# GpSimd's gathers of an item's routed results: one unbroken group, behind a wait for the stacked queries of the item two ahead

## The reference, cut to what matters

```python
x = x + L0_ffn(L0_cond(x))     # pooling, then a mixture of 32 experts, 4 of them for each token
x = x + L1_ffn(L1_cond(x))     # a matrix chosen for each item, attention, then 8 experts, 2 for each token
# L1_ffn.block_forward, for each item:
h = layernorm(x, ln1_g, ln1_b)
q, k, v = split(h @ Wqkv)                       # 16 heads of 16
q, k = (rope(q), rope(k))
probs = softmax(causal(q @ k.T / sqrt(16)))
x = x + (probs @ v) @ Wproj
h2 = layernorm(x, ln2_g, ln2_b)                 # routed to 2 of 8 experts
```

## Time and profile before

| | us |
|---|---|
| median of 3 runs | 1644.0 (1638.05 to 1645.99) |
| the profiled execution, its own time | 1637.33 |
| its span, from the first to the last instruction | 1635.4 |
| TensorE's granted clock, mean over the span | 0.94 |

### The profile page before, as it was taken

How to read it: one execution, slowest core, us unless ns; L and a number is a source line. 1 busy time by engine, 2 the same in 40 slices (tenths; PEclk the granted TensorE clock), 3 DMA queues, 4 the chain that set the end, 5 groups by cost and what they waited for, 6 DMA issues and landing times.

```text
span 1635.4 us, 27565 instructions
## 1 busy us (share of the span) xinstructions
PE 1438.9 (88%) x9777; PEld 1247.0 (76%) x9777; DVE 1028.3 (63%) x2455; ACT 916.5 (56%) x2160; POOL 717.0 (44%) x710
## 2 busy tenths in 40 slices
PE   7997599999999997589978888879965999999996
PEld 5776599999999985466766666667744999999996
DVE  2998376776677767457766766757654555655552
ACT  5886255555555532267766666667844545554552
POOL 0787443344334114344444455553344444544443
PEclk9989799999999999799988999999976999999998
DMA  5411356555655531586576665566743223433312
GB/s 178 136 56 32 84 162 180 154 163 175 180 158 160 150 110 41 97 142 124 117 129 114 117 127 101 103 119 112 110 129 99 72 53 92 98 88 89 52 22 26
DMA packets 139448, 182.00 MB, mean 111 GB/s; under 512 B 22485, under 2 KB 107296, under 8 KB 139312
## 3 DMA queue, kind: packets, MB, share of 16 engines
q1 hardware_dynamic: 110512, 127.23, 31.3%
q0 software_dynamic: 28160, 51.96, 15.7%
q10 hardware_dynamic: 640, 1.05, 0.4%
HBM read 107.28 MB, written 42.08 MB: 91 GB/s over the span
## 4 chain that ended last, share of the span: by engine, by line
PE 64%; DVE 15%; another core or an unknown queue 8%; issue 6%; ACT 3%; POOL 2%; DMA 1%; SPq 1%; ACTq 0%; DVEq 0%; POOLq 0%
PE banks L942 40%; PE banks L1483 4%; PE banks L1440 4%; PE banks L451 3%; PE banks L1536 2%; PE banks L1004 2%; DVE X L1705 2%; DVE rm L1737 2%; DVE hidden L977 2%; DVE smax L1695 2%; PE banks L1496 1%; PE banks L1457 1%; DVE lo_w L911 1%; PE banks L1498 1%
## 5 line engine op out<-in xcount | busy, mean ns | idle before, releaser
L942 PE MATMUL banks<-hi_x,hi_w 128*128 128x320 f32 (+1 forms) x832 | 291.6, 350 | 36.5 <-DVE hidden L977 29.7
L942 PE MATMUL banks<-lo_x,hi_w 128*128 128x320 f32 (+1 forms) x832 | 286.5, 344 | 0.0
L942 PE MATMUL banks<-hi_x,lo_w 128*128 128x320 f32 (+1 forms) x832 | 286.1, 344 | 0.0
L942 PE MATMUL banks<-hi_w,hi_h 128*128 128x256 f32 x896 | 261.5, 292 | 6.8 <-issue 4.5
L884 POOL DMA_INDIRECT xe<-pooled,idx x160 | 155.7, 973 | 228.2 <-PE banks L1004 183.1
L942 PE MATMUL banks<-lo_w,hi_h 128*128 128x256 f32 x896 | 254.4, 284 | 0.0
L942 PE MATMUL banks<-hi_w,lo_h 128*128 128x256 f32 x896 | 254.2, 284 | 0.0
L942 PEld LDWEIGHTS banks<-hi_x,hi_w 128*128 128x128 f32 x832 | 158.9, 191 | 58.7 <-DVE hidden L977 33.4
L1896 POOL DMA_INDIRECT out<-X,tab x64 | 106.3, 1661 | 200.5 <-DVE X L1999 185.8
L1589 ACT ACTIVATE PN<-banks,smax 128x256 f32<-128x256 f32 (+1 forms) x512 | 180.7, 443 | 13.3 <-DVE smax L1695 13.2
L942 PEld LDWEIGHTS banks<-hi_w,hi_h 128*128 128x128 f32 x896 | 172.3, 192 | 8.4 <-issue 5.9
(11 more groups left out here) (187 smaller groups left out, 3100.7 us busy)
## 6 DMA issues: line engine op xcount, KB each, us to landing
w<-in_L_ffn_w SPq DMA_DIRECT2D x96, 256.0 KB, 5.6
done<-res SPq DMA_DIRECT2D x32, 640.0 KB
QS<-parts_qk SPq DMA_DIRECT2D x128, 128.0 KB
BIG<-in_L_ffn_W SPq DMA_DIRECT2D x16, 1024.0 KB
KS<-parts_qk SPq DMA_DIRECT2D x120, 128.0 KB
mask<-in_c_masks SPq DMA_DIRECT2D x16, 257.0 KB, 2.8
pooled<-XF SPq DMA_DIRECT2D x16, 256.0 KB, 3.2
WS<-in_L_cond_W SPq DMA_DIRECT2D x16, 256.0 KB
```

Of the source, the lines that this page charges most:

```text
L942: last = e.matmul(o, a[i], b[j], start=start and k == 0, stop=stop and k == 2, skip_group_check=True)
```

## The change

In `POOL_ROUND` the eight gathers of item i + 3 now stand behind both `entry` pairs, the rotation and `base`: six in one piece, then the two norms with one gather between them, and the last gather behind. Before the first gather of an item b (from the fourth item on) POOL also waits until `s_stack[0]` tells that the queries of item b - 2 have been stacked.

```diff
     POOL_ROUND = (
-        ("got", 2, 1, 3), ("entry", -3, 0), ("entry", -3, 1), ("qk", 1, 0), ("qk", 1, 1), ("entry", -3, 2),
-        ("got", 3, 0, 0), ("got", 3, 0, 1), ("got", 3, 0, 2), ("got", 3, 0, 3), ("entry", -3, 3),
-        ("got", 3, 1, 0), ("got", 3, 1, 1), ("base", -2), ("norm", -1, 1), ("got", 3, 1, 2), ("norm", 2, 0))
+        ("entry", -3, 0), ("entry", -3, 1), ("qk", 1, 0), ("qk", 1, 1), ("entry", -3, 2), ("entry", -3, 3),
+        ("base", -2), ("got", 3, 0, 0), ("got", 3, 0, 1), ("got", 3, 0, 2), ("got", 3, 0, 3), ("got", 3, 1, 0),
+        ("got", 3, 1, 1), ("norm", -1, 1), ("got", 3, 1, 2), ("norm", 2, 0), ("got", 3, 1, 3))
...
                 if b >= NGA and t == 0 and k == 0:
                     e.wait_ge(s_comb, TB * K0 * (b - NGA + 1))
+                if b >= 3 and t == 0 and k == 0:
+
+                    e.wait_ge(s_stack[0], N_STACK * (b - 1))
                 e.indirect_dma_start(
```

## The result

The changed kernel takes **1688.88 us** (median of 3 runs, 1680.68 to 1692.34) against 1644.0: a ratio of 1.028 [1.025, 1.032] (the brackets behind a ratio are its 95% interval), slower by 2.8%. The forecast was 1682. The profiled execution took 1692.34 us, its span is 1690.5, so the span grew by 55.1. Lines behind L1412 have moved down by three: `got` is L1416, `scale` L1663, the division of the outputs L1750.

What follows compares the result with a forecast made beforehand. PE was taken as the bound (busy 88%), POOL's work as costing nothing. Thirteen rounds of 37.0 us less 0.7 make 480.3 against 442.3, +38 us, so 1682; own range 1660 to 1708, 8 in 10 1640 to 1712.

Steps and rivals of the forecast that it cites:

- the two ways named: POOL's order can act only through what its gathers do to others and by making somebody wait for POOL.
- The relief: Second norm's variance ready 9.84 us after Q, the queries' first stacking DMA, in place of 17.9; some 8 us.
- The ring: Queries' first DMA through landing, gathers, norm and `xn` to the next item's queries: 37.0 us a round.
- terms 1 and 2: Queries' stack lands 11.0 us after its first DMA is issued, then POOL's wait ends and it starts: 0.1.
- terms 3 and 4: Six POOL gathers, 7.3 us; then 0.1 to the norm and 3.7 from its start to the end of `xn`.
- terms 5 and 6: End of `xn` to the next queries, 13.7 us, plus PE's results seen late, 1.1 us.
- The late results of PE: At the turning of `xn`, after POOL's unbroken burst: 1.1 us a round, range nothing to 4.1.
- The clock: TensorE waits some 8 us ahead of `norm_turn`; a lower clock may fall on `qk`; only widens the upper end.
- (b): Rival: the round stays at today's 34.0 us, landing 9.5 and no lateness; no change, 1643 us; chance 0.15.
- (c): Rival: queries land as soon as bytes allow, 8.4 us; round 32.4, -22 us, 1622 us; chance 0.12.
- (d): Rival: PE's lateness 4.1 us worse in the unbroken run, half clock over `qk`; round 41, 1734 us; chance 0.05.
- (e): Rival: POOL reaches the new wait after the queries have landed, so it never binds; 1644 us; chance 0.02.

Runs made afterwards that it cites:

- e1: The changed kernel without its new wait, so the new order of POOL's list alone: 1633.13 us, 0.994 of the kernel before.
- e2: The kernel before, in its old order, with only the new wait added ahead of an item's first gather: 1708.02 us, 1.039 of the kernel before.
- e11: Changed kernel with both norms ahead of the wait and all eight gathers, for item i + 4, behind it: 1640.8 us, 1.008 of the kernel before.
- e10: Kernel before with gathers spread out, five kept apart by waits for DVE's row maxima, no wait for the stack: 1595.06 us, 0.980.
- e8: The spread gathers of e6 moved a round ahead (for item i + 4): 1590.74 us, 0.967 of the kernel before.
- e6: Same kernel as e10, made from the kernel before, on the chip without late results: 1551.27 us, 1.033 of the kernel before there.
- e3: Kernel before without the gathers from the fourth item on, old rows added instead: 1546.66 us in a single execution.
- e9: Same kernel as e3, without gathers from the fourth item on, on another chip: 1548.95 us, 0.943 of the kernel before there.
- e5: Same kernel as e11, made from the changed kernel, on the chip without late results: 1561.39 us, 1.042 of the kernel before there.

## Why the prediction was right

**The bound.** POOL does not set the pace by its work; it acted through the two ways named. Removing its gathers altogether, without changing anything that PE has to do, gave 26.85 us a round.

**The relief** was forecast at some 8 us and came: the variance is ready at Q + 10.1 (932.8 less 922.73) in place of Q + 17.9, and "remote" at the division is nothing, forecast under 15.

**The wait spends it.** The norm comes at Q + 18.8 (941.49 less 922.73), forecast Q + 18.5. `e1` and `e2` show that the wait does this: 0.994 without it, 1.039 with it alone. `e11` shows the same from the other side. DVE waits 7.0 to 8.4 us ahead of `scale` in 11 of the 13 rounds, forecast 6 to 9; 9.2 and 11.7 in the other two.

**The ring**, term by term, as means over the 13 rounds. Queries issued until the first gather (terms 1 and 2): 11.9 (11.4 to 13.4), forecast 11.1. From there to the end of `xn` (terms 3 and 4): 10.8, forecast 11.1 (7.3 + 0.1 + 3.7). From `xn` to the next queries (terms 5 and 6): 15.0 (13.9 to 15.8), forecast 13.7 + 1.1 = 14.8. Sum 37.7, forecast 37.0. So the excess over the old period of 34.0 was 3.7 us a round, forecast 3.0. The term that was mis-sized is the landing. I had the keys begin to share the DMA engines at Q + 6; in nine of the 13 rounds they were issued at Q + 5.1. By the prediction's own working, half the rate from there on, the 8.4 us of bytes end at 5.1 + 2 x 3.3 = 11.7, and 11.7 is the mean of those nine. In the other four SP needed longer to issue the queries themselves (5.9 to 6.6 us), and they landed at 11.9 to 13.4; why later, although the keys began later, is not shown. By the Trainium skill, page "DMA: Bandwidth & Descriptors", section "Anatomy of one DMA", an estimate of the landing is Q + 6.7. That section's fit is for DMAs issued by GpSimd, and these are issued by SP. The run disagrees with the estimate, as the rows of before did: the shortest was 11.4.

**The late results of PE** were put at 1.1 us, at the end of the burst; the place is right (`oT`, 3.81 us in the round shown, 40.6 us in ten rounds). ACT does not need `oT` alone there, so not all of it is on the ring: the whole stretch came out 0.2 us over the forecast.

**The clock** had no term. 28% of the time at the lower level, against 18% before (mean 0.91 over the same rounds), is 10.6 us a round in place of 6.1. PE's busy time in the rounds did not grow, which speaks against the clock as the main cause; what it costs inside terms 5 and 6 was not measured by itself.

**The whole.** 13 rounds took 490.0 us against a forecast of 480.3: they grew by 47.6, forecast 38, a fifth short. The profiled execution took 1692.3 against 1675. The rest of that gap, about 7.5 us, lies outside the rounds. The median is only 6.9 above the forecast, and part of that is luck: the prediction put the median 6.7 above the profiled execution, as it was before, and after the change it lay 3.5 below it.

**The rivals.** (b), no change, needed a landing at 9.5 and (c), faster, one under 9.4: no round had it. (d), far slower, needed PE's lateness to add 4 us to every ring; late results of PE showed up in ten of 13, and the stretch as a whole was hardly longer. (e), a wait that never binds, is out: it bound in all 13 rounds, 12.7 us each (forecast 9 to 11, for I had POOL arrive later).

**Open.** Whether the changed kernel gains or loses on the chip where PE's results are not late: it was not run there. The ring needs no lateness, so I would expect a loss, and a larger one in per cent.

## What to carry to other kernels

A new wait in an in-order queue binds everything behind it: follow the queue from the wait to whatever the waited-for event itself depends on, and if that closes a ring, sum the ring and compare it with the present period, because a relief smaller than the ring's excess is lost whole. If transfers of one engine disturb another, look for a place with rests between them before looking for a quiet time to bunch them in: bunched ones gained 0.6% without the wait (`e1`), cost 0.8% with the norms ahead (`e11`) and 2.8% behind the wait (the change), spread ones gained 2.0% (`e10`) and a round ahead 3.3% (`e8`). This held on the chips with late results; on the other one spreading cost 3.3% (`e6`). And run what is compared on the same chip, in one comparison.

## What the runs showed of the hardware

**PE's results are seen late while POOL issues indirect DMAs in close succession.** By the profile a matmul's records end on time (886.03 in the round of the earlier trace rows), and PE goes on to its next ones, but the engines that wait for it start up to 4 to 8 us later, and the profile finds no releaser ("remote"). The ends of matmuls are modelled in the profile, so whether the result itself is late or only the news of it is not shown. In every view of the rounds read here the steps so hit are ones that wait for PE. At the worst step of DVE or ACT it made 16.1 us (`e10`) to 72.0 us (before) in 13 rounds, in every kernel with gathers, on all chips but one, and nothing in `e3` and `e9`, without gathers; cutting the stacking to an eighth left most of it. (In `e8`, `e10` and `e11` SP's queue too has waits ended by "remote", 19.6 to 97.9 us, where it waits for PE's `scores` before a stack.) Why a gather delays PE's results and not those of the others stays open.

**It depends on the chip.** The kernel before takes 1500 us on one chip and 1628 to 1644 on the others, and neither profile of that chip, of `e5` and `e6`, has a "remote" wait. The spread gathers take the same time a round on both kinds, 30.77 and 30.62 us (`e6`, `e10`); those in one piece take 31.85 and 34.05 (`e5`, `e11`). Outside the 13 rounds the profiled executions of these pairs differ by 41.4 and 43.9 us, in the other phases, which gather by indirect DMA too. The kernel before gains 128.1 in all (1628.4 less 1500.28); with 41.4 to 43.9 taken off, 84 to 87 us are left for its rounds, an estimate of 6.5 to 6.7 us a round: most of the 7.2 that the gathers cost elsewhere.

**Stacks within the on-chip memory were slow to land.** Eight DMAs of 128 KB, with eight more behind them, needed 11.4 to 13.4 us; in the round shown the DMA engines moved 123 GB/s up to the landing, and 234 GB/s once the gathers ran with the keys.
